# Gated cross- and self-attention block: queries and keys in two fp16 parts instead of three bf16 parts, row maxima of two heads in 64 array rows each

## The chip, the cores and the metric

The kernel runs on one core of one Trainium2 chip. The metric is the device time of one execution in microseconds; the numbers compared are medians of several runs. A profiled execution has its own time, which is not quite the median.

## The reference, cut to what matters

A batch of B = 4 sequences of L = 512 tokens, width D = 256, 16 heads of 16 dimensions, passes through a gated cross-attention and then a gated block with self-attention and a routed feed-forward net. All in float32; a top-2 choice of experts follows the attention, so scores must keep nearly full float32 precision.

```python
def xattn(query, key, value, ...):                     # query = layernorm(x), key = value = ctx
    q, k, v = heads(query @ wq.T + bq), heads(key @ wk.T + bk), heads(value @ wv.T + bv)
    attn = softmax(einsum('bhld,bhsd->bhls', q, k) / 4, axis=-1)
    return einsum('bhls,bhsd->bhld', attn, v)
def ffn(src, ...):                                     # src = layernorm(x)
    q, k = rope(heads(src @ Wq)), rope(heads(src @ Wk_c @ Wk));  v = heads(src @ Wv_c @ Wv)
    sa = einsum('bhqk,bhkd->bhqd', softmax(q k^T / 4), v) @ Wo
    x = rmsnorm(src + sa)
    ...                                                # shared net and 2 of 8 experts per token
    return rmsnorm(x + shared + routed)
x = x + tanh(g_xattn) * xattn(layernorm(x), ctx, ctx, ...)
x = x + tanh(g_ffn) * ffn(layernorm(x), ...)
```

## The kernel before

The program is written by hand, one instruction list for each engine, tied by semaphores; nothing is scheduled by a compiler. It has three stages: a start (loads, transposed weights, projections of the first two instances), an attention stage, and an end stage (the feed-forward nets and the routing), which the change leaves alone.

**Instances, groups, steps.** There are 8 attention instances (`INST`): cross-attention of the four batches (`"c"`), then self-attention of the four (`"s"`). An instance has 4 groups of 4 heads (`HG`), a group has 16 steps (`STEPS`), a step is one unit: the 128 x 512 score tile of one head and one block of 128 keys. Four steps, one key block, are called a block here. In the order of TensorE (PE), per step: one score matmul (L1653, K rows of the stack `ks` as weights, `qs` moving); at every odd step `max_pair` (L1603), two matmuls that give 128 query rows x 512 scores each, for the row maxima; at every fourth step the value products of the block before (L1629, four heads in four column groups, in two passes each). ScalarE (ACT) turns a score tile into exp (L891). VectorE (DVE) reduces a pair of maximum tiles with one instruction (`row_max`, L1136).

**Stacks.** Products of float32 precision are made of 16-bit parts. Each query and key is split in three bf16 parts (`parts`, in `mix`): the first is a rounded copy (`first_part`, L811, ACT), then the rest is taken (`rest`, L638, GpSimd/POOL), rounded again (`second_part`, L815, ACT), and the third is what is left (`third_part`, L643, POOL). Six products of parts (`Q_PART`, `K_PART`) times 16 dimensions make a contraction of 96 rows (`STK`). SyncE (SP) writes the parts to DRAM (`put`, L516, L522) and reads them back as stacks of 96 rows (L537, L551). Two more rows carry the negated row maximum in two bf16 parts, against rows of ones: the score matmul contracts 98 rows and its result already has the maximum taken off.

**Where the maximum comes from.** `row_max` runs `LEAD` = 12 pairs ahead of the scores, through a ring of two double banks (`Ring`, `ring_emptied`): PE may fill a pair only when the pair two before it is reduced. After the eighth pair of a group DVE makes the two parts (L1144, L1145), PE turns them (`turn_max`, L1610) at step `AT_MAX` = 9, ACT copies them (L784) and at step `AT_ROWS` = 11 issues the DMA that puts them into the stack (`max_rows`, L789). The first score of the next group waits for that DMA. At step 8 (`AT_HEADS`) PE turns the value product of the group before (L1617) and DVE divides it (`heads_out`, L1157, L1158). Scores use three banks in turn (`SCORE_BANKS`); the projection tiles of the next instance take the same three banks.

**Projections of the next instance** are spread over the steps by tables (`CROSS_STEPS`, `SELF_STEPS`, `FA_STEPS`: what, which half or tile, at which step relative to the start of the instance before it). They crowd around the start of an instance; an engine reads from the table what it does after which step.

**The start.** Bias and inputs are loaded; ACT waits for all five bias loads (`s_wb`) before its first copy; keys and queries of instance 0 are split by `begin_parts` (L846) and `begin_rest` (L1101), `later_parts`.

## Time and profile before

| | us |
|---|---|
| median of 3 runs | 789.88 (789.3 to 790.07) |
| profiled execution | 793.59 |
| its span, first to last instruction | 791.8 |

PE is busy in 94% of the span, DVE in 65%, ACT in 52%, POOL in 28%. The attention stage lasts from about 54 us (first score) to about 537 us, the end stage from there to 791.8 us. The time of the attention stage can be read by groups: ACT copies the turned maxima (L784) once in each of its groups, at the same step, so two such rows lie one group apart.

### The profile page before, as it was taken

Reading aid. Unit: us, or ns where it says so; the run is one execution under the profiler, and the core shown is the slowest. Engines: PE = TensorE matmul, PEld = TensorE weight load, DVE = VectorE, ACT = ScalarE, POOL = GpSimd, SP = SyncE. Lnnn points to the kernel's source line nnn. Section 1 sums busy time; section 2 is a strip of 40 time slices with the busy share of each in tenths; the row PEclk is TensorE's granted clock in tenths of the full one; section 3 lists DMA queues with packets and bytes.
Section 4 is the critical chain, followed back from the end, with each engine's and each line's share of the span. In section 5 each row is a group of like instructions: output and inputs, shape, how many; then the busy total and the mean of one; then the engine's idle time right before and its main releaser. Section 6 shows DMA issues by size and latency. Waiting matters only on the chain.

```text
span 791.8 us, 10350 instructions
## 1 busy us (share of the span) xinstructions
PE 746.5 (94%) x3510; PEld 342.7 (43%) x3510; DVE 512.4 (65%) x777; ACT 408.1 (52%) x766; POOL 225.6 (28%) x342
## 2 busy tenths in 40 slices
PE   5889999999999999999999999999999999989994
PEld 3432343243233233233323423425645755458883
DVE  2588847956978878878797798743366022623764
ACT  2437867777767767876675777683211122222000
POOL 3360222314315405304222410010105622400654
PEclk9989999999999999999999999999999999999997
DMA  7792334216215414513411341006003734000010
GB/s 233 207 256 57 81 84 144 79 32 204 63 50 164 122 41 126 141 41 94 146 43 40 125 112 47 1 2 213 0 0 125 272 115 133 0 1 1 34 41 34
DMA packets 51892, 73.31 MB, mean 93 GB/s; under 512 B 7808, under 2 KB 42880, under 8 KB 51840
## 3 DMA queue, kind: packets, MB, share of 16 engines
q1 hardware_dynamic: 47248, 63.80, 27.4%
q0 software_dynamic: 2816, 8.46, 2.8%
q10 hardware_dynamic: 1776, 0.40, 0.3%
q8 instruction: 29, 0.48, 0.3%
q14 instruction: 23, 0.19, 0.1%
HBM read 45.04 MB, written 27.33 MB: 91 GB/s over the span
## 4 chain that ended last, share of the span: by engine, by line
PE 75%; DVE 14%; ACT 5%; issue 3%; DMA 1%; POOL 1%; ACTq 0%; DVEq 0%; POOLq 0%
PE ps L1483 35%; PE ps L1629 12%; PE ps L1653 11%; PE ps L1603 10%; DVE negm L1136 7%; ACT hS L891 3%; PE ps L1478 2%; DVE bst L1014 2%; PE ps L1617 1%; PE ps L1542 1%; DMA bv_bc<-in_L_xattn_bv_dram 1%; PE ps L1537 1%; PE ps L1563 0%; POOL out_dram L753 0%; DVE rows L1021 0%
## 5 line engine op out<-in xcount | busy, mean ns | idle before, releaser
L1136 DVE TENSOR_REDUCE negm<-ps 128x2 f32<-128x1024 f32 x256 | 304.0, 1221 | 75.8 <-PE ps L1603 68.0
L891 ACT ACTIVATE hS<-ps 128x512 f32<-128x512 f32 x512 | 280.6, 604 | 116.2 <-PE ps L1653 114.4
L1653 PE MATMUL ps<-w 98*128 98x512 bf16 x512 | 170.6, 386 | 4.8 <-DVE qk L1069 1.9
L1603 PE MATMUL ps<-w 96*128 96x512 bf16 x512 | 154.9, 383 | 7.3 <-DVE negm L1136 6.4
L1629 PE MATMUL ps<-hS,mix 128*17 128x512 f32 x1024 | 134.7, 598 | 0.2
L1653 PEld LDWEIGHTS ps<-w 98*128 98x128 bf16 x512 | 44.0, 97 | 157.0 <-ACT hS L891 76.7
L1603 PEld LDWEIGHTS ps<-w 96*128 96x128 bf16 x512 | 47.9, 99 | 59.7 <-DVE negm L1136 13.2
L1335 DVE SCALAR_TENSOR_TENSOR ctxs<-qk,ps 128x512 f32<-128x512 f32 x32 | 22.0, 688 | 76.3 <-ACT qk L925 51.1
L925 ACT ACTIVATE qk<-ps 128x512 f32<-128x512 f32 x32 | 19.1, 597 | 82.5 <-PE ps L1483 78.6
L1483 PE MATMUL ps<-w,hS 128*128 x256 | 55.7, 379 | 2.0 <-issue 2.0
L1483 PEld LDWEIGHTS ps<-w,hS 128*128 128x128 f32 x256 | 48.6, 190 | 9.4 <-issue 2.9
L615 POOL TENSOR_TENSOR mdif<-bst 128x4 f32<-128x4 f32 x12 | 2.5, 206 | 156.5 <-DVEq L976 156.5
L653 POOL TENSOR_SCALAR hS<-hS,tg 128x256 f32<-128x256 f32 x16 | 14.9, 931 | 99.6 <-DVEq L1162 99.6
L638 POOL TENSOR_TENSOR qk<-qk,mix 128x1024 f32<-128x1024 f32 x14 | 29.8, 2130 | 42.9 <-ACT mix L811 42.6
L633 POOL TENSOR_TENSOR qk<-qk,hT 128x1024 f32<-128x1024 f32 x8 | 18.8, 2350 | 76.1 <-DVEq L976 76.1
L1629 PEld LDWEIGHTS ps<-hS,mix 128*17 128x17 f32 x1024 | 17.0, 95 | 53.9 <-ACT hS L891 29.9
L643 POOL TENSOR_TENSOR mix<-qk,mix 128x1024 bf16<-128x1024 f32 x14 | 29.9, 2133 | 22.6 <-ACT mix L815 21.6
L1483 PE MATMUL ps<-fout,hS 128*128 128x256 f32 x128 | 30.6, 396 | 1.8 <-issue 1.8
L1483 PE MATMUL ps<-cT,fin 128*128 128x512 f32 x64 | 28.6, 595 | 0.7 <-ACT cT L918 0.7
L725 POOL DMA_INDIRECT scrf<-rows,place x16 | 15.7, 980 | 47.0 <-DVEq L976 42.4
L1338 DVE SCALAR_TENSOR_TENSOR hS<-ctxs,ps 128x512 f32<-128x512 f32 x32 | 22.0, 687 | 10.3 <-PE ps L1483 8.8
L1483 PEld LDWEIGHTS ps<-fout,hS 128*128 128x128 f32 x128 | 25.3, 199 | 7.3 <-issue 3.8
(210 smaller groups left out, 875.5 us busy)
## 6 DMA issues: line engine op xcount, KB each, us to landing
w<-scrq SPq DMA_DIRECT2D x32, 384.0 KB, 4.5
scrk<-mix SPq DMA_DIRECT2D x24, 256.0 KB, 2.1
scrq<-mix SPq DMA_DIRECT2D x16, 384.0 KB, 3.3
scrq<-mix SPq DMA_DIRECT2D x24, 256.0 KB, 2.5
w<-scrk SPq DMA_DIRECT2D x32, 192.0 KB, 2.9
w<-scrk SPq DMA_DIRECT2D x32, 128.0 KB, 2.9
w<-in_L_ffn_W_experts_dram SPq DMA_DIRECT2D x8, 512.0 KB, 8.0
mix<-scrf SPq DMA_DIRECT2D x4, 528.0 KB, 5.5
```

Source lines behind the costliest of these rows:

```text
L633: link(pool.tensor_tensor(qk[X][:], qk[X][:], rb[X], ALU.add))
L638: link(pool.tensor_tensor(qk[X][:], qk[X][:], parts[X][:, 0], ALU.subtract))
L643: link(pool.tensor_tensor(parts[X][:, 2], qk[X][:], parts[X][:, 1], ALU.subtract))
L891: nc.scalar.activation(prob[:, kt % PROB_SLOTS, s % HG, :], slot_bank(("unit", u)), ACT.Exp, scale=SC).then_inc(s_exp, 1)
L925: nc.scalar.activation(th[k % 4], end_full(f"{name}{b}", 2 * p), ACT.Tanh, scale=0.5).then_inc(s_th, 1)
L1136: V.tensor_reduce(negm[:, gi % 2, h, 2 * t2:2 * t2 + 2], ps[:, bank:bank + 2, :], AX.X, ALU.max, negate=True).then_inc(s_re, 1)
L1335: V.scalar_tensor_tensor(out=uu[:, k % 2, :], in0=th[k % 4], scalar=1.0, in1=end_full(f"{name}{b}", 2 * p), op0=ALU.add, op1=ALU.mult).the ...
L1338: V.scalar_tensor_tensor(out=hS[:, b * TT:(b + 1) * TT, p, :], in0=uu[:, k % 2, :].rearrange("p (t j) -> p t j", t=TT), scalar=0.5, in1=en ...
L1483: last = MM(o, w, r, start=(j == 0), stop=(j == len(terms) - 1))
L1603: last = MM(ps[:, bank + t, :], qs[0:STK, g, h, tt * P:(tt + 1) * P], ks[0:STK, g, h, :], start=True, stop=True)
L1629: last = MM(ps[32 * h:32 * h + VM, 6, :], vp[n % 2][:, kt, g * HG + h, :], prob[:, kk % PROB_SLOTS, h, :], start=(kt == 0), stop=(kt == TT ...
L1653: MM(take(("unit", u)), ks[:, g, h, kt * P:(kt + 1) * P], qs[:, g, h, :], start=True, stop=True).then_inc(s_sT, 1)
```

## The change

Every query and key is scaled by a power of two so that it fits fp16, then split in two fp16 parts. Three products of parts replace six, and the contraction is 48 rows, 50 with the maximum. Two heads of a group now lie one above the other: heads 0 and 2 in partitions 0 to 49, heads 1 and 3 in partitions 64 to 113 (`HALF` = 64).

- `max_pair`: its two matmuls are for two heads, one in each half of the array's rows, in two banks; before, they were two query blocks of one head. Score matmuls stay one a step, alternating halves from head to head.
- The second and third parts go (ACT L815, POOL L643); POOL's one subtraction gives the second part. Stacks are half as large, DRAM traffic for them too, and the loads per group and operand are two.
- The scale: DVE takes maxima of absolute values of inputs, weights and biases (`magnitudes`), ACT writes them to DRAM (`put_magnitudes`), waits, and reads them back broadcast to all partitions (`get_magnitudes`); DVE makes bounds and powers of two (`powers`, a chain of some ten small instructions). Four times: at the start for batches 0 and 1, at steps -41 to -26 of the tables for batches 2 and 3 (batch 2 with the self-attention's weights as well).
- exp takes its scale from a column `esc` of SBUF, no longer from a constant; bias and scale of the query and key copies come from `bfit` and `fit`.
- The DMA of the maximum row is issued by SP, twice (one for each half), behind SP's other DMAs and waits in an order written out by step; `AT_MAX` is 11, `AT_COPY` 3, `LEAD` 14. The step tables are new.

```diff
-NTERM = 6
-NPART = 3
-Q_PART = [0, 0, 0, 1, 1, 2]
-K_PART = [0, 1, 2, 0, 1, 0]
-LEAD = 12
+NTERM = 3
+NPART = 2
+Q_PART = [0, 0, 1]
+K_PART = [0, 1, 0]
+HALF = 64
+LEAD = 14
-AT_COPY, AT_HEADS, AT_MAX, AT_ROWS = 4, 8, 9, 11
+AT_COPY, AT_HEADS, AT_MAX, AT_ROWS = 3, 8, 11, 11
...
-    CROSS_STEPS = [("stats", 0, -34), ("norm", 1, -20), ("norm", 0, -16), ("tile", 2, -12), ("empty", 2, -12), ("tile", 0, -11),
+    CROSS_STEPS = [("mags", 0, -41), ("put", 0, -33), ("get", 0, -32), ("stats", 0, -32), ("powers", 0, -26),
...
+            def max_rows(gi):
+                sp.wait_ge(s_mts, gi + 1)
+                n_ = MPART * HP * TT
+                for j in range(2):
+                    sp.dma_start(qs[j][STK:KROWS, gi % NG, :, :], mTs[j * n_:(j + 1) * n_, gi % 2, :]).then_inc(s_mrow, 16)
...
+            def get_magnitudes(e):
+                n_ = EVENTS[e][1]
+                act.wait_ge(s_mst, 16 * (e + 1))
+                ge(act, s_fit, e)
+                act.dma_start(amall[:, 0:P * n_], scra[e].rearrange("p n -> (p n)").unsqueeze(0).to_broadcast([P, P * n_])).then_inc(s_mld, 16)
...
                         nc.scalar.activation(prob[:, kt % PROB_SLOTS, s % HG, :], slot_bank(("unit", u)),
-                                             ACT.Exp, scale=SC).then_inc(s_exp, 1)
+                                             ACT.Exp, scale=esc[:, e:e + 1]).then_inc(s_exp, 1)
...
+            def powers(e):
+                c, n_ = EVENTS[e]
+                dve.wait_ge(s_mld, 16 * (e + 1))
+                link(V.tensor_reduce(amx[:, c:c + n_], amall[:, 0:P * n_].rearrange("p (q n) -> p n q", n=n_), AX.X, ALU.max))
...
-                for t in range(2):
-                    tt = 2 * t2 + t
-                    last = MM(ps[:, bank + t, :], qs[0:STK, g, h, tt * P:(tt + 1) * P], ks[0:STK, g, h, :],
+                for j in range(2):
+                    last = MM(ps[:, bank + j, :], qs[j][0:STK, g, hp, tt * P:(tt + 1) * P], ks[j][0:STK, g, hp, :],
                               start=True, stop=True)
...
-                        MM(take(("unit", u)), ks[:, g, h, kt * P:(kt + 1) * P], qs[:, g, h, :],
+                        MM(take(("unit", u)), ks[h % 2][:, g, h // 2, kt * P:(kt + 1) * P], qs[h % 2][:, g, h // 2, :],
```

PE, the end of a group of instance 0 and the first score of the next group. `exp_done` is ACT's exp three tiles back, `ring_emptied` the reduction two pairs back, `maximum_parts` DVE's parts, `maximum_rows` the landed maximum row. Before:

```order
L1653 MATMUL ps<-w 128x512 [waits exp_done]
L1603 MATMUL ps<-w 128x512 [waits ring_emptied,stack_loaded3]
L1603 MATMUL ps<-w 128x512
L1610 MATMUL ps<-identb,m 128x128 [waits exp_done,maximum_parts]
L1653 MATMUL ps<-w 128x512 [waits exp_done] x2
L1603 MATMUL ps<-w 128x512 [waits ring_emptied]
L1603 MATMUL ps<-w 128x512
L1629 MATMUL ps<-hS,mix 17x512 [waits exp_done]
L1629 MATMUL ps<-hS,mix 17x512 x3
L1653 MATMUL ps<-w 128x512 [waits turned_maximum_copied]
```

And now, from the pair before the turned maximum:

```order
L1700 MATMUL ps<-w 128x512 [waits ring_emptied]
L1700 MATMUL ps<-w 128x512
L1726 MATMUL ps<-hS,mix 17x512 [waits exp_done]
L1726 MATMUL ps<-hS,mix 17x512 x3
L1707 MATMUL ps<-identh,m 128x128 [waits exp_done,maximum_parts]
L1749 MATMUL ps<-w 128x512 [waits exp_done] x2
L1700 MATMUL ps<-w 128x512 [waits ring_emptied]
L1700 MATMUL ps<-w 128x512
L1749 MATMUL ps<-w 128x512 [waits turned_maximum_copied]
```

The turned maximum moved behind the value products of step 11: two scores, a pair, two scores, a pair and one block of value products now lie between it and the score that waits for its row; before, one such block and two scores with a pair more.

SP, around the end of instance 1's fourth group, as it stands now (before, SP issued no maximum rows; they were on ACT's queue):

```order
L561 DMA scrq<-mix 128x2x512 [waits stack_loaded3,stack_loaded2,first_part_ready0,stack_loaded1,stack_loaded0]
L561 DMA scrq<-mix 128x2x512
L575 DMA w<-mTs 2x8x128 [waits turned_maximum_copied]
L575 DMA w<-mTs 2x8x128
L556 DMA scrq<-mix 128x2x512 [waits stack_loaded3,stack_loaded2,parts_ready0,stack_loaded1,stack_loaded0]
```

The two halves of the maximum row (`w<-mTs`) stand behind two writes of a first part, and so behind that part's wait.

ACT, in instance 0, where the maxima of batch 2 and of the self-attention's weights go out and come back; before there was none of it:

```order
L942 ACTIVATE hS<-ps,esc 128x512 [waits score_full] x3
L829 DMA scra<-am 128x4 [waits magnitudes_ready]
L942 ACTIVATE hS<-ps,esc 128x512 [waits value_product,score_full]
L836 DMA w<-scra 128x512 [waits powers_ready,magnitudes_stored]
L942 ACTIVATE hS<-ps,esc 128x512 [waits score_full] x3
```

One exp lies between the write to DRAM and the load that waits for it; the exps behind it wait too.

## Rows read from the trace of the kernel before

**Rows 1.** The page: busy us, share of the span, instructions, by engine.

```profile
PE 746.5 (94%) x3510; PEld 342.7 (43%) x3510; DVE 512.4 (65%) x777; ACT 408.1 (52%) x766; POOL 225.6 (28%) x342
```

**Rows 2.** Stretches: us, busy and instructions by engine, granted clock, DMA share, GB/s.

```profile
54.00:60.00 6.00, 6.00 (x17) 2.22 (x16) 4.79 (x5) 3.42 (x7) 3.98 (x56) 0.57 1.03 343
126.20:138.20 12.00, 12.00 (x70) 3.58 (x69) 10.26 (x13) 9.14 (x20) 3.79 (x3) 1.00 0.40 122
349.00:371.50 22.50, 22.02 (x94) 7.86 (x93) 16.93 (x20) 12.17 (x24) 6.83 (x3) 1.00 0.24 69
```

**Rows 3.** Timeline of one light group: start us, us, engine, line, operation, count.

```profile
128.12 0.60 PE L1653 MATMUL ps<-w 98*128 98x512 bf16 x2
128.56 0.60 PE L1603 MATMUL ps<-w 96*128 96x512 bf16 x2
129.20 2.36 DVE L1136 TENSOR_REDUCE negm<-ps 128x2 f32<-128x1024 f32 x2 [0.41 <-PE ps L1603]
129.96 1.05 PE L1629 MATMUL ps<-hS,mix 128*17 128x512 f32 x8
130.94 0.60 PE L1653 MATMUL ps<-w 98*128 98x512 bf16 x2
131.37 2.06 ACT L891 ACTIVATE hS<-ps 128x512 f32<-128x512 f32 x4 [0.76 <-PE ps L1653]
```

**Rows 4.** Timeline, ACT's copies of the turned maximum, one a group.

```profile
102.29 0.26 ACT L784 ACTIVATE mTs<-ps 32x128 bf16<-32x128 bf16 x1
126.22 0.26 ACT L784 ACTIVATE mTs<-ps 32x128 bf16<-32x128 bf16 x1
138.16 0.26 ACT L784 ACTIVATE mTs<-ps 32x128 bf16<-32x128 bf16 x1
151.02 0.26 ACT L784 ACTIVATE mTs<-ps 32x128 bf16<-32x128 bf16 x1
165.10 0.26 ACT L784 ACTIVATE mTs<-ps 32x128 bf16<-32x128 bf16 x1
...
349.01 0.27 ACT L784 ACTIVATE mTs<-ps 32x128 bf16<-32x128 bf16 x1
371.47 0.25 ACT L784 ACTIVATE mTs<-ps 32x128 bf16<-32x128 bf16 x1
388.38 0.26 ACT L784 ACTIVATE mTs<-ps 32x128 bf16<-32x128 bf16 x1
```

**Rows 5.** Timeline, DVE back to back, and its work between two groups' maxima.

```profile
64.19 4.62 DVE L1136 TENSOR_REDUCE negm<-ps 128x2 f32<-128x1024 f32 x4
79.46 1.40 DVE L1014 BATCH_NORM_STATS2 bst<-rows 128x6 f32<-128x256 f32 x4
137.23 0.17 DVE L1144 CAST m<-negm 128x16 bf16<-128x16 f32 x1
138.62 2.36 DVE L1136 TENSOR_REDUCE negm<-ps 128x2 f32<-128x1024 f32 x2
```

**Rows 6.** Groups by line and shape: xcount, busy us, mean ns, idle before.

```profile
L825 ACT ACTIVATE qk<-ps,bqk 128x512 f32<-128x512 f32 x12 | 8.2, 687 | 19.4 <-PE ps L1483 17.0 <-PE ps L1563 2.5
L830 ACT ACTIVATE nT<-ps 128x512 f32<-128x512 f32 x8 | 4.9, 610 | 0.0
```

**Rows 7.** Timeline without maxima, at the stage's end: one block of exps.

```profile
526.30 2.07 ACT L891 ACTIVATE hS<-ps 128x512 f32<-128x512 f32 x4 [0.32 <-PE ps L1653]
```

**Rows 8.** Timeline, the DMA of the maximum row as ACT issues it.

```profile
126.81 0.62 ACTq L789 DMA_DIRECT2D w<-mTs  x1
```

**Rows 9.** DMA queues between 128.0 and 128.4 us: queue, packets, MB, share.

```profile
q10 hardware_dynamic: 34, 0.01, 9.2%
```

**Rows 10.** Timeline of the start: ACT's first copy and first parts, PE's first pair.

```profile
11.36 1.08 ACT L820 ACTIVATE cT<-ps 128x512 f32<-128x512 f32 x2 [2.45 <-DMA bv_bc<-in_L_xattn_bv_dram]
16.32 0.69 ACT L846 ACTIVATE mix<-ps,bqk 128x512 bf16<-128x512 f32 x1 [1.92 <-PE ps L1483]
52.53 2.17 PE L1603 MATMUL ps<-w 96*128 96x512 bf16 x4 [2.38 <-DVE negm L1136]
```

408 lines of the change are left out of this document (240 added, 168 removed).

## The prediction

> **What bounds the kernel now.** The page first [rows 1]: PE is busy in 94% of the span, DVE in 65%. That is an average over stages, so the busy time by stretches comes next [rows 2]: in a light group (one with no projection in it), 126.2 to 138.2 us, PE is busy for all 12.00 us, DVE for 10.26, ACT for 9.14. Then the timeline of such a group [rows 3]: blocks of four steps start at 128.12 and 130.94, 2.82 us apart. In a block PE runs four scores, four maximum matmuls and the value products. Four 16-bit matmuls fill the stretch from 128.12 to 129.00, so one is 0.22 us; eight are 1.73 (at 0.216), and the value products 1.05: 2.78 of the 2.82. PE is the bound, by its own work and not by a wait. The time of a group is read off the copies of the turned maximum [rows 4]: light 11.94 us (126.22 to 138.16), with row statistics 12.86, with three input tiles 14.08, across the start of an instance, where most projections stand, 23.93 (cross) and 22.46 (self, 349.01 to 371.47), with an output projection 16.91.
>
> **What the side by side maxima take away.** Two maximum matmuls of a pair now use different halves of the array's rows and different banks, and wait for one semaphore. No row tile is in this trace, but its column counterpart is: the value products are eight matmuls (four heads, two passes) in 1.05 us [rows 3], where eight of 0.216 in a row would be 1.73 or more. So I take the second of a pair as free, 0.216 us a pair; the bounds are 0 (they run one after the other) and 0.216. A group has 8 pairs: 1.73 us. PE's own work in a light group falls from 11.94 to 10.21.
>
> **What is late next.** DVE. Reductions back to back are 4.62 us for four, a first one of 1.23 and 1.13 for each more [rows 5]: eight are 9.14. From the end of the last reduction (the 0.17 us row starts at 137.23) to the next one at 138.62 lie 1.39 us of parts and head division [rows 5]; split over two places now, 0.1 more. So a light group costs DVE 10.65 us, more than PE's 10.21. The ring is two pairs deep, so neither engine absorbs much of the other's hitches: I add 0.25 for that, 10.9 to 11.1. The gain in a light group is 0.9 us, not 1.73.
>
> **exp with its scale from SBUF.** An ACT copy of a 128x512 tile with a column operand is 687 ns, without one 610 [rows 6]. exp now has one such operand: 16 of them cost about 0.08 each, 1.2 us a group, and ACT's 9.14 [rows 2] become 10.4, just below DVE. Without maxima at all, a block of exps is 2.07 with 0.32 idle in front [rows 7], 2.39 a block or 9.6 a group; that is the floor of the loop of scores, exps and values today, and the dearer exps fill its idle time. In the sum this is nothing but part of the 0.25; at worst it is 0.3 to 0.6 us a group.
> The Trainium skill, "ScalarE: Activation LUTs", section "What ACT_TABLE_LOAD costs", states about 93 ns for each column operand: a rule against this change. By it ACT would carry 1.5 us more a group where the rows say 1.2; the trace is 15 ns under it.
>
> **Group by group.** From the tables of steps I count, between the second copy of a turned maximum and the last one, 30 groups:
> - 6 across the start of an instance (2 of 23.93, 4 of 22.46). PE is the bound with projections of some 12 us; DVE is busy 16.93 in 22.5 [rows 2]. The gain is at least 1.73. Where two scores stand next to each other, in different halves, they can overlap too, if both their waits are met, for 1.73 more. But the projections now stand in larger lumps (three tiles at step -3), behind which DVE has only two pairs in hand, so between lumps DVE sets the pace. I take 2.2 each: 13.2.
> - 3 with an output projection (16.91): DVE needs 10.65 and 1.4 for statistics [rows 5] and some 1.4 for the added tiles, 13.5. 1.9 each: 5.7.
> - 5 with three input tiles (the first 14.08; the self ones are read as 13.46 in the same view): PE 11.8 to 12.4. 1.8 each: 9.2.
> - 4 light ones, 0.85 each: 3.4.
> - 4 with statistics (12.86): DVE 10.65 + 1.40 = 12.05, with hitches 12.3. 0.35 each: 1.4.
> - 4 of self instances with two sets of statistics or a norm on DVE: 2.7 together.
> - 4 that carry magnitudes and powers. DVE adds one reduction of 128x1024 (1.2), for batch 2 three weights too (1.1), a reduction of 128x512 (0.6) and 10 to 15 chained small instructions of 0.17 and up [rows 5], 1.7 to 2.4. ACT waits for its own DMA to DRAM between step -33 and -32: queued behind are exps, behind them PE's scores. A DMA lands 1.2 to 1.6 us after its issue (below); three score banks hide one exp of that; 1 us each. Together they end 7.0 later than now (range 4 to 10).
>
> Sum: 13.2 + 5.7 + 9.2 + 3.4 + 1.4 + 2.7 - 7.0 = 28.6 us less.
>
> **The maximum row.** Its DMA was issued at 126.81 and its packets moved between 128.0 and 128.4 [rows 8, 9]: 1.6 us. Now the turn is two steps later and behind a block of value products. From its end PE still has four scores and two pairs (1.3 us) and a block of values (1.05), 2.35, before it wants the row; ACT's copy (0.26), SP's two issues (about 0.4 each) and 1.6 make 2.6. A wait of 0.2 to 0.3, which DVE's backlog covers. At the end of instance 1 the row also stands behind writes of a first part; PE has projections to run there.
>
> **POOL and the other copies.** The third part (POOL), the second rounding (ACT) and half of the DMA bytes leave engines that nobody waits for: nothing, covered by PE's and DVE's work.
>
> **The start.** ACT no longer waits for the value bias, which held its first copy to 11.36 [rows 10]; but the first parts, now at 16.32, wait for a chain: maxima of inputs, weights and biases (my estimate: done at 9.5 to 11, behind loads that ACT's first copy waited for until 11.36 [rows 10]), store, broadcast load, powers. With 1.6 [rows 8, 9] to 3 us for each DMA, since others are in flight, and 2.5 for the powers it ends at 15.5 to 19.5. One part less to make gives 2 us back. Net +1, from -2 to +4. `LEAD` 14 puts two more reductions (2.3) before the first score and takes two out of the end; there the dearer exps add 22 x 0.08 = 1.8. I take +3.3 for both, with slow clock (below).
>
> **Forecast.** 28.6 - 1 - 3.3 = 24.3 us less: the span 791.8 becomes 767.5, and the median 789.88, which lies 3.7 below the profiled execution's 793.59, becomes about **765.5 us**.
>
> **The rivals.**
> - *Scores overlap wherever they are neighbours, and DVE never starves.* For it: nothing but their own waits keeps them apart. Then PE's light group is 8.5 us, the groups at instance starts fall by up to 3.4, those with an output projection by 2.9. 6 x 1.2 + 3 x 1.0 + 5 x 0.9 = 14.7 less: **751 us**.
> The Trainium skill, "TensorE: Matmul & The Clock Gate", section "Part 3: Packing small matmuls — row/col tiling", says that matmuls in distinct row groups run concurrently; this rival is that rule in full, and no row of the trace has row tiles to show it.
> - *ACT becomes the bound.* With 0.1 an exp and its loop with PE closed (the 0.32 idle of [rows 7] stays), a light group is 9.6 + 1.6 and more, 11.5. Twenty groups lose 0.5: **776 us**.
> - *The maximum row comes late (the side of slower).* SP issues it behind waits and behind stack loads and writes of up to 1 MB on the same queue. It decides from 24.3 / 31 = 0.8 us of real stall a group; at 1.2 a group the kernel takes **802 us**. Against it: the 2.6 us above, and that stack loads stand at step 1 of a group, ten steps earlier.
> - *The halves do not overlap at all.* PE stays at 11.94 a group; only start, powers and lead remain, partly hidden: **796 us**.
> - *The clock falls.* After a wait of 2.38 us for DVE, four maximum matmuls took 2.17 [rows 10] (0.43 past the first; 1.2 GHz), and from 54 to 60 us the granted clock was 0.57 [rows 2]. PE will be 80 to 95% busy in light groups; with 12.00 of 12.00 [rows 2] it kept 2.4 GHz. Groups at half the rate would be near 20 us, after which PE is fully busy again; ten such groups are 80 us.
>
> **How the numbers follow.** Forecast 0.47, full overlap 0.18, ACT 0.15, late row 0.09, no overlap 0.07, clock 0.04. About 0.2% (1.6 us) is what a measurement can tell from no change. Faster: the first three and a little of the others, 0.84; within 0.2%: 0.03; slower: 0.13. The forecast's own unknowns are 4 on the start, 3 on the powers, 4 on the hitches of 30 groups. 8 in 10 reach from below the full overlap's 751 to above ACT's 776: 744 to 784.
>
> **What would show it.** PE's maximum pairs: two in about 0.4 us from start to end, not 0.60. Light groups at 10.9 to 11.1 between turned maxima; 10.65 would say that DVE never starves, 11.5 with ACT filled that ACT bounds, 11.9 that PE still does. ACT's exps at 690 ns. DVE's idle time named by PE in projection groups only. Score waits for `maximum_rows` under 0.3 us. First parts at 15.5 to 19.5 us. What would make the forecast wrong: a granted clock below 1.00 in the attention stage, or scores that wait for the row.

## The result, and the profile after

The changed kernel takes **820.8 us** (815.1 to 821.9 in four runs), the kernel before, run beside it, 789.6 us: a ratio of 1.039, 95% interval 1.033 to 1.044. It is slower by 31 us, where 24 us less were forecast. The profiled execution has a span of 818.8 us against 791.8, 27.0 more. In the experiments below, a run over 1.5% above the fastest of its kernel is named with its clock and is no part of the ratio.

The page of the changed kernel, to be held against [rows 1]: busy time by engine, the granted clock in forty slices, and the groups of exps and scores.

```profile
PE 717.9 (88%) x3510; PEld 309.8 (38%) x3510; DVE 525.1 (64%) x827; ACT 441.6 (54%) x753; POOL 191.3 (23%) x327
...
PEclk9785999979999589999999999997999999999998
...
L942 ACT ACTIVATE hS<-ps,esc 128x512 f32<-128x512 f32 x512 | 317.6, 690 | 71.3 <-PE ps L1749 63.0
...
L1749 PE MATMUL ps<-w 50*128 50x512 f16 x512 | 166.1, 410 | 34.9 <-ACT hS L942 30.2
```

PE has less to do (718 us, not 746) and is idle for 12% of the span instead of 6%. The clock row has slices of 0.5 to 0.8 in the attention stage (61 to 82, 164 to 184 and 266 to 307 us, and 552 to 573 at its end). The same row of the kernel before:

```profile
PEclk9989999999999999999999999999999999999997
```

Where the 27.0 us are can be counted with the copies of the turned maximum. These are ACT's rows of the changed kernel for some of the groups that [rows 4] and the prediction speak of (the copies now stand at step 11 of a group, not 9).

```profile
111.33 0.27 ACT L823 ACTIVATE mTs<-ps 32x128 f16<-32x128 f16 x1 [1.09 <-PE ps L1707]
129.63 0.27 ACT L823 ACTIVATE mTs<-ps 32x128 f16<-32x128 f16 x1 [0.26 <-PE ps L1707]
147.64 0.27 ACT L823 ACTIVATE mTs<-ps 32x128 f16<-32x128 f16 x1 [0.18 <-PE ps L1707]
...
341.96 0.25 ACT L823 ACTIVATE mTs<-ps 32x128 f16<-32x128 f16 x1
354.87 0.27 ACT L823 ACTIVATE mTs<-ps 32x128 f16<-32x128 f16 x1 [0.18 <-PE ps L1707]
367.24 0.27 ACT L823 ACTIVATE mTs<-ps 32x128 f16<-32x128 f16 x1
380.44 0.27 ACT L823 ACTIVATE mTs<-ps 32x128 f16<-32x128 f16 x1 [0.19 <-PE ps L1707]
401.32 0.25 ACT L823 ACTIVATE mTs<-ps 32x128 f16<-32x128 f16 x1
...
510.09 0.27 ACT L823 ACTIVATE mTs<-ps 32x128 f16<-32x128 f16 x1 [0.18 <-PE ps L1707]
521.74 0.27 ACT L823 ACTIVATE mTs<-ps 32x128 f16<-32x128 f16 x1 [0.18 <-PE ps L1707]
```

And one row of the kernel before that [rows 4] does not have:

```profile
88.20 0.26 ACT L784 ACTIVATE mTs<-ps 32x128 bf16<-32x128 bf16 x1
```

Each kernel has 32 copies and so 31 intervals between them.

| stretch | before | after | difference |
|---|---|---|---|
| start, to the first copy | 49.8 | 62.9 | +13.1 |
| intervals 1 to 3 | 38.4 | 48.5 | +10.1 |
| interval 7 (fourth store of magnitudes) | 12.9 | 19.6 | +6.7 |
| intervals 13 and 14 (half clock, 270 to 290 us) | 34.6 | 42.5 | +7.9 |
| the other 25 intervals | 386.4 | 375.7 | -10.7 |
| after the last copy | 269.8 | 269.7 | -0.1 |

Single intervals mislead where the step tables changed. In a cross instance three of the ten projection tiles now stand ahead of the copy that they stood behind. So interval 5, across the start of an instance, fell from 23.93 to 18.01 us, but interval 4 rose from 14.09 to 18.30; the two together fell only from 38.02 to 36.31, and intervals 8 and 9 from 38.02 to 36.10. The forecast had 26 us and more for the 25 intervals (five starts at 2.2, three output projections at 1.9, five groups with three tiles at 1.8, and the lighter groups): 10.7 came, and four places give back more than three times as much. Single kinds of group, in undisturbed stretches at full clock:

| interval | before | forecast | after |
|---|---|---|---|
| light group | 11.9 | 10.9 to 11.1 | 11.65 |
| three input tiles (self) | 13.46 | 11.7 | 13.20 |
| start of a self instance | 22.46 | 20.3 | 20.88 |
| the group behind it | 12.1 | - | 12.91 |

The last two belong together, since the copy has moved by two steps: 34.6 before, 33.8 after.

Stretches of the changed kernel, in the order of [rows 2], for the second and the fourth of the four places:

```profile
60.00:80.00 20.00, 15.32 (x61) 3.27 (x60) 19.09 (x29) 7.42 (x13) 4.04 (x56) 0.63 0.24 80
90.00:110.00 20.00, 13.59 (x92) 3.44 (x89) 18.84 (x38) 14.10 (x25) 5.35 (x13) 0.99 0.16 34
261.00:270.00 9.00, 6.27 (x38) 1.56 (x34) 7.96 (x10) 6.86 (x11) 4.16 (x3) 0.99 0.17 55
270.00:290.00 20.00, 19.73 (x72) 5.53 (x76) 10.90 (x13) 11.91 (x21) 4.31 (x4) 0.50 0.37 114
```

Interval 1 runs in large part at half clock. In intervals 2 and 3 the clock is nearly whole (0.99 at 90 to 110 us), DVE is busy for 18.84 of 20 us and PE only for 13.59; DVE there makes the magnitudes and powers of batch 2 besides the row maxima. Before the fall at 270 us PE was busy for 6.27 of 9 us; in the fall it is busy for 19.73 of 20.

The cause of the losses at the start and in interval 7 stands in the timeline of the changed kernel. There are four stores of magnitudes, at 9.66, 32.40, 96.93 and 161.49 us. ACTq rows are DMAs as ACT issues them; brackets give the idle time ahead and what ended it.

```profile
9.66 0.34 ACTq L829 DMA_DIRECT2D scra<-am  x1
...
16.59 0.33 ACTq L836 DMA_DIRECT2D w<-scra  x1
...
19.88 1.28 DVE L1094 TENSOR_REDUCE amx<-w 128x5 f32<-128x640 f32 x1 [8.75 <-DMA w<-scra]
...
22.87 1.45 ACT L893 ACTIVATE mix<-ps,bfit,fit 128x512 f16<-128x512 f32 x2 [4.82 <-DVEq L1027]
...
161.49 0.33 ACTq L829 DMA_DIRECT2D scra<-am  x1
...
169.28 0.33 ACTq L836 DMA_DIRECT2D w<-scra  x1
169.65 1.84 ACT L942 ACTIVATE hS<-ps,esc 128x512 f32<-128x512 f32 x3 [5.83 <-DMA scra<-am]
170.39 0.10 PEld L1749 LDWEIGHTS ps<-w 50*128 50x128 f16 x1 [5.85 <-ACT hS L942]
```

The store of a few bytes per partition takes 6.9 us at the start (9.66 to 16.59) and 7.8 us at 161 us; the load 3.3. ACT waits in order, so at 161 us its exps stand behind the store, and PE's scores behind those. The first parts come at 22.9 us, in the kernel before at 16.3 [rows 10]. The second store, at 32.4 us, took 8.8 us in the same way; the third, at 96.9 us, landed in 1.5.

The packets are not what takes so long. ACT's DMA queue between 162.2 and 162.6 us:

```profile
q10 hardware_dynamic: 144, 0.00, 19.2%
```

All packets of the store of 161.49 are in these 0.4 us, and the store counts as landed only at 169.3; those of the second store had all moved by 33.5 us, and it landed at 41.2. The third store had the same neighbours as the fourth (four stack loads of SP, issued just behind it) and landed in 1.5. What fills the time between packets and landing is open.

Last, one block of a light group, to be held against [rows 3].

```profile
218.37 0.10 PEld L1749 LDWEIGHTS ps<-w 50*128 50x128 f16 x2 [0.99 <-DMA w<-mTs]
218.37 0.39 PE L1749 MATMUL ps<-w 50*128 50x512 f16 x2
...
218.60 0.38 PE L1700 MATMUL ps<-w 48*128 48x512 f16 x2
...
218.80 2.42 ACT L942 ACTIVATE hS<-ps,esc 128x512 f32<-128x512 f32 x4 [0.41 <-PE ps L1749]
...
219.54 0.39 PE L1749 MATMUL ps<-w 50*128 50x512 f16 x1 [0.34 <-ACT hS L942]
219.54 0.60 PE L1700 MATMUL ps<-w 48*128 48x512 f16 x2
220.07 1.05 PE L1726 MATMUL ps<-hS,mix 128*17 128x512 f32 x8
...
221.06 0.39 PE L1749 MATMUL ps<-w 50*128 50x512 f16 x2
```

Two neighbours in different halves take 0.38 to 0.39 us from start to end, scores and maxima alike; [rows 3] had 0.60. The overlap is there. But the block is 2.69 us (218.37 to 221.06) where it was 2.82, and PE waits in it: the fourth score needs the bank that the first exp reads. The block is a loop: score 0.43, exp 0.69, 0.05, fourth score with its pair 0.53, values 0.99.

### The profile page after: what moved, and what is told of

It reads as the page before. It is cut to its first block, busy times and chain, and to the rows that moved or that the text cites. A ratio compares the mean times of both kernels' runs of the same rounds, so it can differ in the third digit from the quotient of the medians.

```text
span 818.8 us, 10431 instructions
## 1 busy us (share of the span) xinstructions
PE 717.9 (88%) x3510; PEld 309.8 (38%) x3510; DVE 525.1 (64%) x827; ACT 441.6 (54%) x753; POOL 191.3 (23%) x327
## 4 chain that ended last, share of the span: by engine, by line
PE 58%; DVE 16%; ACT 11%; DMA 6%; issue 5%; POOL 2%; ACTq 0%; SPq 0%; DVEq 0%; POOLq 0%
PE ps L1581 30%; PE ps L1726 10%; ACT hS L942 8%; DVE negm L1229 7%; PE ps L1749 7%; PE ps L1700 4%; DMA scra<-am 3%; POOL scrf L761 2%; PE ps L1576 2%; PE ps L1714 2%; PE ps L1640 1%; PE ps L1635 1%; DVE hS L1250 1%; DMA w<-mTs 1%; ACT rows L844 1%
## 5 line engine op out<-in xcount | busy, mean ns | idle before, releaser
L942 ACT ACTIVATE hS<-ps,esc 128x512 f32<-128x512 f32 x512 | 317.6, 690 | 71.3 <-PE ps L1749 63.0
L1749 PE MATMUL ps<-w 50*128 50x512 f16 x512 | 166.1, 410 | 34.9 <-ACT hS L942 30.2
L1700 PE MATMUL ps<-w 48*128 48x512 f16 x512 | 137.2, 406 | 14.1 <-DVE negm L1229 9.9
L1726 PE MATMUL ps<-hS,mix 128*17 128x512 f32 x1024 | 145.7, 643 | 0.4 <-ACT hS L942 0.4
L1749 PEld LDWEIGHTS ps<-w 50*128 50x128 f16 x512 | 39.8, 95 | 195.1 <-ACT hS L942 112.3
L694 POOL TENSOR_SCALAR hS<-hS,tg 128x256 f32<-128x256 f32 x16 | 14.9, 929 | 151.9 <-DVEq L1254 151.9
L1700 PEld LDWEIGHTS ps<-w 48*128 48x128 f16 x512 | 28.1, 95 | 40.3 <-DVE negm L1229 17.9
L684 POOL TENSOR_TENSOR mix<-qk,mix 128x1024 f16<-128x1024 f32 x14 | 29.8, 2127 | 50.5 <-ACT mix L858 49.8
L1581 PE MATMUL ps<-rope_sb,fin 128*128 128x512 f32 x64 | 28.2, 593 | 0.0
L1581 PE MATMUL ps<-wT,fin 128*128 128x512 f32 x64 | 28.1, 592 | 0.0
L1714 PE MATMUL ps<-identf,oT 128*128 128x128 f32 x128 | 22.6, 303 | 6.1 <-DVE negm L1229 5.3
```

The costliest lines, as they stand in the source:

```text
L684: link(pool.tensor_tensor(parts[X][:, 1], qk[X][:], parts[X][:, 0], ALU.subtract))
L942: nc.scalar.activation(prob[:, kt % PROB_SLOTS, s % HG, :], slot_bank(("unit", u)), ACT.Exp, scale=esc[:, e:e + 1]).then_inc(s_exp, 1)
L1581: last = MM(o, w, r, start=(j == 0), stop=(j == len(terms) - 1))
L1700: last = MM(ps[:, bank + j, :], qs[j][0:STK, g, hp, tt * P:(tt + 1) * P], ks[j][0:STK, g, hp, :], start=True, stop=True)
L1714: last = TR(ps[:, bank, tt * P:(tt + 1) * P], oT[:, tt * P:(tt + 1) * P], identf[:])
L1726: last = MM(ps[32 * h:32 * h + VM, 6, :], vp[n % 2][:, kt, g * HG + h, :], prob[:, kk % PROB_SLOTS, h, :], start=(kt == 0), stop=(kt == TT ...
```

## The experiments

All run beside the kernel before, each time on the same chip; ratios are to its runs.

**The changed kernel without the round trips.**

```
-                act.dma_start(scra[e], am[:, c:c + n_], ...).then_inc(s_mst, 16)
-                act.wait_ge(s_mst, 16 * (e + 1))
-                act.dma_start(amall[:, 0:P * n_], scra[e]...).then_inc(s_mld, 16)
+            pool.memset(amall, 1.0).then_inc(s_mld, 64)
```

> The changed kernel without the two DMAs of each magnitudes event (no store of am, no broadcast load, no wait for either); the gathered magnitudes are a memset of 1.0. It leaves out that the bounds come from data; the reductions, the small operations of powers() and everything behind them stay. Theory A (the loss sits mainly in the DMA round trips, for which ACT and DVE wait in order): the first parts go from 22.9 us to about 16, the first turned maximum from 62.9 back to 49 to 52, the 5.8 us wait of ACT at 165 us goes, and with it most of the low clock behind it: 790 to 797 us, 24 to 31 less than the changed kernel. Rival B (the score, exp and values loop is the loss; the start is later for another reason, the greater LEAD and the chain of parts): 812 to 817. Rival C (only the clock counts): the clock would fall elsewhere and the time stay within 5 us of 821.

795.6 us, ratio 1.010 (1.005 to 1.015): 25 us less than the changed kernel by the medians, 17 to 28 by the ratios. First parts at 13.8 us, first copy of a turned maximum at 44.8 (before: 49.8): this alone is 18.1 of the 25.5 us between the two profiled spans. Interval 7 falls from 19.6 to 14.9 us. Intervals 13 and 14 are 34.4 us, since the clock did not fall there this time, which the edit need not have caused. Theory A's number; B and C are out for this part. But intervals 1 to 3 still take 48.0 us, so the round trips are not what they lose by. The clock rises only to 0.943 to 0.960 (the changed kernel: 0.940 to 0.952).

**exp's scale as a number.**

```
-                                             ACT.Exp, scale=esc[:, e:e + 1]).then_inc(s_exp, 1)
+                                             ACT.Exp, scale=SC * 2.0 ** -9).then_inc(s_exp, 1)
```

> The changed kernel with the scale of exp as a number in the instruction instead of a column of esc; it leaves out that this scale follows the bounds. exp falls from 690 to about 605 ns, 512 of them. Theory A (in groups without projections the loop score, exp, score, values sets the pace, in which one to four exps of a block stand): 0.09 to 0.36 us a block, 128 blocks, less where projections bound: 6 to 20 us less, 801 to 815. Rival B (DVE bounds the light groups, as forecast): under 3 us less. Rival C (the maximum row's landing bounds each group, so a shorter loop only waits longer for it): under 3 us less too, with the wait of scores for mTs grown by what the loop saves.

823.4 us, with three of four runs at a clock of 0.92 to 0.93 (822.7 to 826.6 us) and one at 0.95 that took 810.3. No verdict: the clock hides the effect. The same edit stands on a steadier kernel below.

**The maximum row four steps earlier.**

```
-AT_COPY, AT_HEADS, AT_MAX, AT_ROWS = 3, 8, 11, 11
+AT_COPY, AT_HEADS, AT_MAX, AT_ROWS = 3, 8, 7, 7
```

> The changed kernel with the turned maximum and its DMAs at step 7 of a group instead of 11. The maxima are ready by step 4 or so in the trace, since LEAD is 14. Theory A (1.0 us of wait for the row at each of most group boundaries): 10 to 20 us less, 801 to 811, and light groups of 10.7 instead of 11.7. Rival B (the wait for the row only takes the place of another, of exps or of DVE's backlog): under 4 us less, light groups stay above 11.3. Rival C (the row's DMAs then meet the stack's writes and loads on SP's queue, issued around steps 1 to 7, and land no earlier): no change or up to 5 us more.

813.9 us, ratio 1.033 (1.027 to 1.039), whose interval overlaps the changed kernel's. The waits of the weight loads of scores for the row, in the changed kernel and then in this one (us in total, times, longest):

```profile
PEld ps L1749 <- DMA w<-mTs: 22.0, 22, 1.4
```

```profile
PEld ps L1749 <- DMA w<-mTs: 1.1, 1, 1.1
```

21 us of wait are gone and 7 us of the median, which the two intervals do not tell from nothing. A light group is 11.51, not 11.65; the start of a self instance with the group behind it is 33.6 (19.4 and 14.2), not 33.8 (20.9 and 12.9), the copy having moved by four steps. Of the rivals B fits best: most of that wait only took the place of another. Its bound of 4 us can be neither kept nor broken by these runs.

**Everything from one half.**

```
-qs[j][0:STK, g, hp, tt * P:(tt + 1) * P], ks[j][0:STK, g, hp, :]
+qs[0][0:STK, g, hp, tt * P:(tt + 1) * P], ks[0][0:STK, g, hp, :]
-ks[h % 2][:, g, h // 2, kt * P:(kt + 1) * P], qs[h % 2][:, g, h // 2, :]
+ks[0][:, g, h // 2, kt * P:(kt + 1) * P], qs[0][:, g, h // 2, :]
```

> The changed kernel with all maxima and all scores computed from the rows of half 0 (so the heads of half 1 are left out and half 0 is done twice); as many matmuls, weight loads and waits as before, but no two neighbours in different halves. Theory A (the overlap is real, 0.2 us a pair of maxima and of scores, and shows where PE is the bound): pairs at 0.60 instead of 0.39, 12 to 35 us more, 833 to 856, most of it in groups with projections. Rival B (the loop of ACT hides what PE saves, so the change has no gain at all to give): within 5 us of 821.

907.1 us (one run: 925.6 at a clock of 0.857), ratio 1.146 (1.138 to 1.153). Neither theory had this number. At full clock a light group took 12.58 us against 11.65, so the overlap is worth 0.93 us there; the rest is the clock. This is 65 us of the attention stage in one row (stretch, length, busy by engine, granted clock, DMA share, GB/s):

```profile
80.00:145.00 65.00, 65.00 (x205) 16.56 (x203) 36.58 (x55) 34.98 (x60) 6.08 (x14) 0.52 0.09 23
```

PE is busy in all of it, and the clock is 0.52. A clock that follows only whether PE is busy cannot do that. What differs from the kernel before, which was as busy at 1.00, is that each maximum or score matmul works on 48 or 50 rows of the array instead of 96 or 98.

**The kernel before on half of its rows.**

```
-qs[0:STK, g, h, tt * P:(tt + 1) * P], ks[0:STK, g, h, :]
+qs[0:48, g, h, tt * P:(tt + 1) * P], ks[0:48, g, h, :]
-MM(take(("unit", u)), ks[:, g, h, kt * P:(kt + 1) * P], qs[:, g, h, :],
+MM(take(("unit", u)), ks[0:50, g, h, kt * P:(kt + 1) * P], qs[0:50, g, h, :],
```

> The kernel BEFORE, with its maxima computed on 48 of their 96 rows and its scores on 50 of their 98 (it leaves out half of the terms and the maximum row); waits, counts, order and every other instruction are as before. It asks why the changed kernel's clock is low (0.94 against 0.986) and why it stayed at half for 60 us in the run on one half although PE was never idle there. Theory D (the granted clock follows how much of the array is at work, and a matmul on 48 or 50 rows counts for half of one on 98): granted clock of the run 0.95 or less, stretches of 10 us and more at 0.5 with PE busy throughout, 800 us or more. Rival E (the clock follows only whether PE is busy): PE's times at full clock do not depend on rows, so nothing changes: clock 0.985, 787 to 791 us.

860.3 us (one run: 887.0 at a clock of 0.880), ratio 1.089 (1.087 to 1.091), clock 0.911 to 0.913 where the kernel before had 0.985 to 0.992. Stretches of this kernel:

```profile
80.00:100.00 20.00, 20.00 (x62) 4.70 (x64) 11.29 (x16) 8.62 (x17) 4.41 (x12) 0.50 0.15 41
100.00:120.00 20.00, 20.00 (x64) 4.52 (x57) 9.22 (x11) 8.68 (x17) 1.66 (x2) 0.50 0.12 30
...
360.00:380.00 20.00, 18.72 (x100) 5.97 (x98) 17.35 (x20) 14.70 (x26) 10.61 (x6) 1.00 0.44 131
```

One edit that touches no wait and no count costs 71 us. Both kernels lose clock between 40 and 60 us, where PE waits for DVE ([rows 2] shows 0.57 for the kernel before); the kernel before was back at 1.00 by 60 us, this one only between 130 and 140, and it was at 0.50 again from 280 to 330. At 360 to 380 us it holds 1.00 with PE less busy (18.72 of 20) than at 80 to 120. Theory D is shown for this kernel: **the rows at work count**. The Trainium skill, "TensorE: Matmul & The Clock Gate", section "Part 1: The HAM clock gate (the "warmup" mystery)", has the clock follow how busy PE has been and says nothing of rows; here the measurement decides.

**The repair: bounds gathered on PE, row early.** A transpose puts each magnitude's 128 values in one row, DVE reduces it, and a matmul of ones with the diagonal of the maxima spreads them. Events 2 and 3 keep their DMAs, with the load issued eleven steps behind the store.

```
+                TR(ps[0:n_, 5, 256 * e:256 * e + P], am[:, c:c + n_], identf[:]).then_inc(s_gt, 1)
+                link(V.tensor_reduce(mx1[0:n_, e:e + 1], ps[0:n_, 5, 256 * e:256 * e + P], AX.X, ALU.max))
+                mark(V.tensor_scalar(dg[0:n_, e, 0:n_], identf[0:n_, 0:n_], mx1[0:n_, e:e + 1], None, ALU.mult))
+                MM(ps[:, 5, 256 * e + P:256 * e + P + n_], g1[0:n_, :], dg[0:n_, e, 0:n_], ...).then_inc(s_mld, 16)
...
-("get", 0, -32), ("stats", 0, -32), ("powers", 0, -26)
+("stats", 0, -32), ("get", 0, -22), ("powers", 0, -15)
-AT_COPY, AT_HEADS, AT_MAX, AT_ROWS = 3, 8, 11, 11
+AT_COPY, AT_HEADS, AT_MAX, AT_ROWS = 3, 8, 7, 7
```

> The changed kernel with all of its computation, and the maxima of magnitudes of the first two events gathered over the partitions by TensorE (a transpose, a reduction of one row, a matmul with a diagonal) instead of by two DMAs; for events 2 and 3 the broadcast load is issued ten steps after the store instead of one, the powers eleven steps later; the turned maximum at step 7. Theory A: the first parts at 15 to 16 us, first turned maximum at 49 to 51, no wait of ACT for a store: as the run without round trips or a little under it by the earlier row: 787 to 797 us. Rival B (the gain of that run came from constant bounds, so other powers, or from a reduction that need not wait): 805 or more. Rival D (rows of the array and the clock are what costs now): the time stays between 790 and 800 with a granted clock of 0.96.

792.4 us, ratio 1.002 (0.998 to 1.006). The chain at its start:

```profile
9.89 0.27 PE L1661 MATMUL ps<-identf,am 128*5 128x128 f32 x1
...
12.41 0.38 PE L1666 MATMUL ps<-dg,g 5*128 5x5 f32 x2
...
14.70 1.45 ACT L898 ACTIVATE mix<-ps,bfit,fit 128x512 f16<-128x512 f32 x2 [3.35 <-DVEq L1027]
```

From the transpose (9.89) to the first parts (14.70) are 4.8 us, where the two DMAs and what follows took 13.2 (9.66 to 22.87). Rival B is out: with bounds from data the time is that of the run with constant ones, or a little less (the earlier row is in this run too). Intervals 1 to 3 are 39.5 us here, not 48.5; which of the run's changes does it was not tried apart. Clock 0.951 to 0.968: D's number too.

**All three left out at once.** The edits of the first three runs together.

> The changed kernel without the round trips (bounds a memset of 1.0), with exp's scale a number, and with the turned maximum at step 7; it leaves out that bounds and scale come from data. What is left is the overlap and the halves alone. Theory A (loop of exps and the row cost 4 to 10 us each on their own): 775 to 788 us. Theory D (whatever makes PE wait less often in a light group is taken back by the clock): 788 to 798 us with a granted clock of 0.95 to 0.96, as without the round trips alone.

782.0 us, ratio 0.991 (0.986 to 0.996), 13.5 below the run without round trips. Theory A; the clock stays at 0.957 to 0.974, near what D says, but does not take everything back.

**More columns in the value matmuls.**

```
-ps[32 * h:32 * h + VM, 6, :], vp[n % 2][:, kt, g * HG + h, :]
+ps[32 * h:32 * h + w_, 6, :], vp[n % 2].rearrange("p t h d -> p (t h d)")[:, at_:at_ + w_]
```

> The changed kernel with 32 columns of stationary values in place of 17 in the value matmuls (the other 15 are the next head's, and nobody reads their rows of the result), so that more of the array's columns are at work in the same time; all of the computation stays. Theory D, if columns count as rows do: granted clock 0.96 or more and 800 to 815 us. Rival E (the clock follows whether PE is busy): clock 0.94 to 0.95, 815 to 822 us. A weight load of 32 columns may take longer than one of 17 (96 ns); it lies beside other work.

826.3 us, ratio 1.047 (1.044 to 1.051), clock 0.928 to 0.940 where the changed kernel had 0.940 to 0.952. No help: with 32 columns for 17 the clock did not rise.

**More rows, on the repaired kernel.**

```
-        qs = [stacks[HALF * j:HALF * j + KROWS, 0] for j in range(2)]
+        qs = [stacks[HALF * j:HALF * j + HALF, 0] for j in range(2)]
+            link(pool.memset(stacks[:, 0], 0.0))
```

(`ks` in the same way; in the first of the two runs the maxima too, and that run leaves out the maximum, whose row it writes as zero.)

> The run e6 (bounds on PE, row early) with both the maxima and the scores on all 64 rows of a half instead of 48 and 50; the added rows are zero in the queries, and the maximum row is written as zero, so the kernel leaves out the maximum. As many instructions, the same waits. Theory D (the granted clock follows the rows at work): clock 0.98 or more against 0.951 to 0.968 of e6, and 776 to 786 us. Rival E (rows do not matter at this point, only PE's idle time does): as e6, 786 to 794.

The first of the two, all matmuls on 64 rows: 778.2 us, ratio 0.987 (0.983 to 0.991), clock 0.983 to 0.989.

> The run e6 with the scores alone on 64 rows of a half instead of 50 (added rows are zero, all of the computation stays); the maxima stay on 48. Theory D: half the effect of e9, clock 0.965 to 0.98, 780 to 790 us, so that it may be the first version under the kernel before. Rival E: as e6, 786 to 794.

780.5 us (one run: 788.7 at a clock of 0.968), ratio 0.987 (0.983 to 0.991), clock 0.981 to 0.985. With nothing but fourteen rows of zeros under each score the repaired kernel gains 12 us (7 to 16) and is faster than the kernel before. The same stretch, first of the repaired kernel on 50 rows, then on 64:

```profile
290.00:310.00 20.00, 18.86 (x69) 5.00 (x69) 13.00 (x16) 12.08 (x21) 9.01 (x6) 0.58 0.30 99
```

```profile
290.00:310.00 20.00, 17.26 (x97) 5.39 (x96) 17.24 (x20) 14.41 (x24) 10.62 (x6) 1.00 0.27 87
```

PE is busier in the first and yet at half clock for most of it. Rival E is out here. The maxima's rows add nothing that can be told.

**The column operand, on the repaired kernel** (50 rows; the edit of the second run).

> The run e6 with exp's scale a number in the instruction; it leaves out that the scale follows the bounds. Without the disturbance of the long start, it prices the column operand: 512 exps of 0.086 us are 44 us of ACT. Theory A (the loop score, exp, score, values sets the pace of light groups): 5 to 12 us less than e6, 778 to 786. Rival B (DVE or PE bounds, as forecast: part of 0.25 us a group): under 4 us less.

777.1 us, ratio 0.983 (0.978 to 0.988): 15 us less than with the column (10 to 20), more than either theory gave. The clock is 0.958 to 0.980, not 0.951 to 0.968, so a part of the 15 may be the clock's; the next run is free of that.

**The column operand, in the kernel before.**

```
-                                             ACT.Exp, scale=SC).then_inc(s_exp, 1)
+                                             ACT.Exp, scale=escc[:, 0:1]).then_inc(s_exp, 1)
```

> The kernel BEFORE with exp's scale read from a column that holds the same number; all of the computation stays. exp goes from 604 to 690 ns. The prediction's step (exps are hidden while PE bounds): within 3 us of the kernel before, 788 to 792. Rival (the loop of scores, exps and values shows even under a PE that is never idle): 4 us or more slower.

803.9 us, ratio 1.019 (1.015 to 1.022), clock as before (0.988): 15 us (12 to 17), where my step said nothing. A block of a light group in this kernel:

```profile
133.06 0.60 PE L1657 MATMUL ps<-w 98*128 98x512 bf16 x2
133.49 2.42 ACT L894 ACTIVATE hS<-ps,escc 128x512 f32<-128x512 f32 x4 [0.49 <-PE ps L1657]
133.50 0.60 PE L1607 MATMUL ps<-w 96*128 96x512 bf16 x2
...
134.22 0.10 PEld L1657 LDWEIGHTS ps<-w 98*128 98x128 bf16 x1 [0.41 <-ACT hS L894]
...
134.46 0.60 PE L1607 MATMUL ps<-w 96*128 96x512 bf16 x2
...
134.98 1.05 PE L1633 MATMUL ps<-hS,mix 128*17 128x512 f32 x8
...
135.97 0.60 PE L1657 MATMUL ps<-w 98*128 98x512 bf16 x2
```

It is 2.91 us long: score 0.43, exp 0.69, 0.06 to the fourth score, 0.22, pair 0.52, values 0.99. With an exp of 0.60 the same terms are 2.82, to the hundredth the block of the kernel before. **The kernel before ran in that loop already**; PE's own work of 2.78 was 0.04 shorter, and the fourth score's wait for the bank (here on PEld) shows as no idle time of PE, since the matmul ahead was counted as still running.

**Breaking the loop: the second pair ahead of the fourth score.**

```
+                        if h == 3 and q < N_PAIRS:
+                            max_pair(q)
                         MM(take(("unit", u)), ...).then_inc(s_sT, 1)
-                        if s % 2 and q < N_PAIRS:
+                        if s % 2 and h != 3 and q < N_PAIRS:
                             max_pair(q)
```

> The run e10 (bounds on PE, row early, scores on 64 rows; complete) with the second maxima pair of each block issued before the block's fourth score instead of behind it. In the trace of the changed kernel a block is the loop 0.42 (score) + 0.69 (exp 1) + 0.05 + 0.54 (fourth score and pair) + 0.98 (values) = 2.68 us, since the fourth score needs the bank that the first exp reads. Theory F (that loop, not PE's work, sets the pace): the pair then runs while exp 1 does, a block is 2.45 to 2.5 (DVE's two reductions 2.36, ACT's four exps 2.42), light groups 10.6 to 10.9 instead of 11.5, 760 to 772 us. Rival B (DVE or the ring of two pairs bounds already): within 4 us of e10, 777 to 784, with PE's wait for DVE grown.

775.7 us, ratio 0.983 (0.980 to 0.986), the fastest of the versions that compute everything. A block in this kernel:

```profile
196.13 0.39 PE L1783 MATMUL ps<-w 64*128 64x512 f16 x2
...
196.57 0.38 PE L1783 MATMUL ps<-w 64*128 64x512 f16 x1
197.10 0.10 PEld L1731 LDWEIGHTS ps<-w 48*128 48x128 f16 x2 [0.65 <-DVE negm L1242]
...
197.64 1.05 PE L1757 MATMUL ps<-hS,mix 128*17 128x512 f32 x8
...
198.63 0.39 PE L1783 MATMUL ps<-w 64*128 64x512 f16 x2
```

The block is 2.50 us, as theory F says, and the second pair now waits for DVE. But a light group falls only from 11.51 to 11.20, and the whole by 5 us, which the two intervals do not tell from nothing (760 to 772 was expected). Below 2.5 us DVE is next, as rival B has it, and one group (386 to 404 us) lost 3 us to a clock of 0.81 again.

**The value products ahead of the fourth score instead.**

```
+                        if h == 3 and (kt or gi):
+                            values(*((gi, kt - 1) if kt else (gi - 1, TT - 1)))
                         MM(take(("unit", u)), ...).then_inc(s_sT, 1)
...
-                        if h == 3 and (kt or gi):
-                            values(*((gi, kt - 1) if kt else (gi - 1, TT - 1)))
```

> The run e10 (complete) with the value products of the block before issued before the block's fourth score, not behind it and the pair. Theory F: they take 1.05 us and fill the wait for exp 1 (0.5 us) and more, so the fourth score comes 0.5 us later, and exp 4 has to wait for it; a block is then 4 scores and 2 pairs at 0.2 to 0.4 each and the values, 2.5 to 2.65: light groups 10.7 to 11.2, 765 to 776 us, less good than e13. Rival B: within 4 us of e10.

785.5 us (one run: 792.7 at a clock of 0.968), ratio 0.995 (0.993 to 0.998): 5 us slower than with them where they were, at a clock of 0.970 to 0.983, not 0.981 to 0.985. Theory F's time failed here. In the profile light groups did fall, to 11.1 to 11.5; the starts of self instances rose from 19.4 to 20.5, but the groups behind them fell by more, and the two together from 33.6 to 33.4. Two groups (24 and 28) are 2.3 and 2.0 us longer, in stretches at a clock of 0.91 and 0.89: most of what the execution lost. Whether the order of instructions brings the lower clock was not tried apart.

**The second pair ahead, in the kernel before with the column** (the pair's edit and the column's, together).

> The kernel BEFORE with exp's scale in a column (as e12, 15 us slower than the kernel before) and with the second maxima pair of each block ahead of the fourth score. A block of the kernel before is the same loop: 0.43 + 0.60 + 0.06 + 0.22 + 0.52 + 0.99 = 2.82, with the column 2.91. Theory F: the pair moves beside exp 1, the loop is 2.4, and PE's own work (2.78) bounds again: the 15 us come back, 784 to 792 us. Rival G (the column's cost is something else, as ACT's own load in the crowded groups): 798 to 804.

800.0 us, ratio 1.015 (1.012 to 1.017). The blocks are 2.82 again (130.03, 132.85, 135.68 in its timeline) and a light group 11.73, under the 11.94 of the kernel before: in light groups the loop was the cause. But a self group with three input tiles takes 14.65, against 14.24 with the column alone and 13.46 in the kernel before. From the first to the last copy of a turned maximum the column had added 11.4 us, and 9.1 of them stay, in groups where ACT also normalises and copies tiles: rival G's time, for the larger part. That ACT's own load does it was not tried apart, nor the new order without the column, which may cost something itself (14.65 where the column alone has 14.24).

**More rows, on the changed kernel as it stands** (scores on 64 rows, by the edit shown for the repaired kernel).

> The changed kernel with its scores on 64 rows of a half instead of 50 (the added rows are zero; complete), nothing else but the clearing of those rows at the start, which nobody waits for. Theory D (rows at work decide the clock here too): granted clock 0.955 to 0.97 and 802 to 812 us, 10 to 18 less than the changed kernel. Rival E (in the changed kernel the clock falls at the waits for the round trips and stays down whatever the rows): under 5 us less, clock 0.94 to 0.95.

814.7 us, ratio 1.032 (1.027 to 1.037), clock 0.942 to 0.965. Between the two expectations, and within the intervals of no change. For the changed kernel as it stands theory D is therefore not shown; what share of its 31 us is clock alone is not settled.

## Why the prediction was wrong, point by point

- **The overlap: right.** Two maxima, and two scores, in 0.38 to 0.39 us; 0.2 us a pair, as taken from the value products. What the prediction cites for it from the Trainium skill, "TensorE: Matmul & The Clock Gate", section "Part 3: Packing small matmuls — row/col tiling" (distinct row groups run concurrently), agrees with these rows.
- **What is late next: wrong.** I took PE's work (2.78 of 2.82) as the bound and DVE as the next one. The bound was the loop of three score banks. Of the 0.43 us a block that the overlap saves, the pair that stands in the loop gives 0.21, and the dearer exp takes 0.09 back: 0.12, where 0.13 was measured (2.82 to 2.69). Light groups gained 0.3 instead of 0.9. I had the row for it: [rows 7] is that loop without maxima, and I wrote that the dearer exps "fill its idle time".
- **exp's column: the largest mis-sized term of the steady part.** The price of one was right (690 ns measured, 604 before, 0.086 more). "In the sum this is nothing but part of the 0.25; at worst it is 0.3 to 0.6 us a group" was worth 15 us in both kernels, nearly 0.5 a group. The rival on ACT (chance 0.15, 776 us) had part of the mechanism, the closed loop with PE.
- **The magnitudes: the step that failed worst.** "A DMA lands 1.2 to 1.6 us after its issue" was read from the packets of one DMA (34 packets, [rows 8, 9]), and packets are not landing: the fourth store's had moved within 1.1 us of its issue, and it landed after 7.8. For the start I allowed 1.6 to 3 us a DMA. The stores took 6.9, 8.8 and 7.8 us and once 1.5 to landing. I gave the start +1 us (-2 to +4) and lead and dearer exps +3.3 together (the start alone measured +13.1), and ACT's wait 1 us each (measured 5.8 at the fourth). I had named the waiting engine and the queue behind it, so only the duration was off, by a factor of two to five; without the round trips the kernel is 25 us faster.
- **The maximum row: size wrong, harmless.** Not 0.2 to 0.3 but 1.0 us at 22 groups; when this wait was taken away, the median fell by 7 us, not by 22.
- **The clock: too small a chance, and half of the reason.** I gave 0.04 to a fall that idle time of PE would cause, to be over once PE is fully busy. The fall is real (0.94 against 0.986), and the one at 270 us does follow a stretch in which PE was busy for 6.27 of 9 us. But then PE was busy for 19.73 of 20 us and the clock stayed at 0.50. In the kernel before and in the repaired one the rows at work per matmul, which the change halves, are what makes that last; in the changed kernel itself this is not shown.
- **The work of magnitudes on DVE.** I took 7.0 us for the four groups that carry it, ACT's waits included (4 to 10). Intervals 2, 3, 6 and 7 are 12.7 us longer: 5.6 of it in intervals 2 and 3, where ACT never waited for a store.
- **The sum.** 821 less 25 for round trips, 15 for the column and 12 for the rows (the last two measured on the repaired kernel) is 769, near the 765.5 of the forecast. That is luck in good part. No run has all three, and the forecast's gains are not there even in the repaired kernel with exp's scale a number: a light group gains 0.7 us (11.94 to 11.24; forecast 0.85), a self group with three tiles 0.6 (13.46 to 12.87; forecast 1.8), the start of a self instance with the group behind it 1.2 (34.6 to 33.4; forecast 2.2 for the start alone). What stands against that is the start: its first copy comes at 46.2 us, 3.6 before that of the kernel before, where I had added 1, and 3.3 more for lead and dearer exps. The sum itself has a small slip too: five groups at 1.8 are 9.0, not 9.2.

## What to carry to other kernels

A busy engine is not yet the bound: before pricing what is taken from it, add up the loop that reuses each buffer (here score, exp, score, pair, values over three banks) and see whether it has the same length. Exchange small values between partitions on an engine, or give their DMAs ten microseconds and a queue on which nobody waits in order. Splitting a tall matmul into two short ones side by side can bring the clock down (0.986 to 0.913 when only the rows were halved); padding with rows of zeros can pay (12 us on the repaired kernel). And when tables of steps change, compare sums of neighbouring groups, not single ones.

## What the runs showed of the hardware

- With PE busy 20.00 of 20.00 us on maxima and scores of 48 and 50 rows the granted clock stayed at 0.50 (1.2 GHz), for 70 us on end, where the same program on 96 and 98 rows was back at 1.00 (2.4 GHz) by 60 us. Rows 50 to 63 filled with zeros raised the clock of the repaired kernel from 0.951 to 0.968 up to 0.981 to 0.985. With 32 columns for 17 in the value matmuls it did not rise (0.928 to 0.940, against 0.940 to 0.952). Why the clock recovers in one place and not in the other is open.
- A store of 4 to 20 bytes from each of 128 partitions to DRAM landed 1.5 to 8.8 us after its issue and held ACT, which waited for it, for up to 5.8 us. Of the 7.8 us of the store at 161.49 its packets account for the first 1.1. The maximum row, two DMAs of 16 rows issued by SP in 1.28 us, landed 2.4 us after the first issue.
- Two 16-bit matmuls of 512 columns in different halves of the rows: 0.38 to 0.39 us together, 0.60 one after the other.
